# Six half-precision matmuls on a constant ahead of each group of neighbour sums

## The reference, cut to what matters

```python
for l in range(2):                       # relational network
    W = einsum('rb,bio->rio', coeff[l], basis[l])      # 8 matrices of 256x256
    msg = (h @ W)[etype, src] * norm                   # one row per edge
    h = segment_sum(msg, dst) + bias[l]                # relu after l == 0
x = layernorm(x + h)
h = x @ W_in + b_in
for l in range(3):                       # mean network
    h = relu(segment_mean(h[src], dst) @ W_agg[l] + h @ W_self[l] + b_hid[l])
out = layernorm(x + h @ W_out + b_out)
```

## Time and profile before

| what | value |
|---|---|
| median of 3 runs | 2405.6 us (2405.01 to 2408.9) |
| profiled execution, its own time | 2384.24 us |
| its span, first to last instruction | 2382.4 us |
| mean granted TensorE clock | 0.891 of full speed |
| busy: TensorE matmul, VectorE, GpSimd, ScalarE | 1794.9, 1202.8, 1254.7, 623.9 us |

### The profile page before, as it was taken

How to read it: one execution, slowest core, us unless ns; L and a number is a source line. 1 busy time by engine, 2 the same in 40 slices (tenths; PEclk the granted TensorE clock), 3 DMA queues, 4 the chain that set the end, 5 groups by cost and what they waited for, 6 DMA issues and landing times.

```text
span 2382.4 us, 29813 instructions
## 1 busy us (share of the span) xinstructions
PE 1794.9 (75%) x7693; PEld 1344.2 (56%) x7693; DVE 1202.8 (50%) x3964; ACT 623.9 (26%) x1520; POOL 1254.7 (53%) x1298
## 2 busy tenths in 40 slices
PE   3747777777677677757777777676676779999997
PEld 2435555555455455535555555455565567777776
DVE  4837745454455544335554555553368743232355
ACT  1112222222222222212322322322112124633332
POOL 5766666666666666366666666666666630000000
PEclk9978879989988898969798888988888889999999
DMA  6333333333333333233333333334533320000011
GB/s 199 87 91 98 101 98 98 100 101 98 102 97 99 101 98 99 65 95 100 104 103 101 103 103 100 104 102 121 171 105 100 95 59 11 1 1 1 1 35 44
DMA packets 118334, 208.03 MB, mean 87 GB/s; under 512 B 53668, under 2 KB 73908, under 8 KB 118168
## 3 DMA queue, kind: packets, MB, share of 16 engines
q0 software_dynamic: 62016, 169.04, 24.9%
q1 hardware_dynamic: 48848, 26.08, 3.8%
q10 hardware_dynamic: 7304, 10.96, 1.4%
HBM read 188.85 MB, written 17.13 MB: 86 GB/s over the span
## 4 chain that ended last, share of the span: by engine, by line
PE 49%; another core or an unknown queue 17%; DVE 14%; issue 13%; ACT 3%; DVEq 2%; POOL 1%; DMA 0%; ACTq 0%; SPq 0%; POOLq 0%
PE bank L657 15%; PE bank L823 11%; PE bank L610 9%; PE bank L645 4%; DVE RY L450 4%; DVE RY L441 3%; PE bank L588 2%; PE bank L840 2%; PE bank L768 2%; DVE RY L376 1%; DVE RY L375 1%; ACT RY L555 1%; ACT RY L489 1%; POOL RY L246 1%
## 5 line engine op out<-in xcount | busy, mean ns | idle before, releaser
L657 PE MATMUL bank<-RY 128*128 128x256 f32 x2580 | 870.6, 433 | 56.4 <-DVE RY L450 43.1
L246 POOL DMA_INDIRECT RY<-H,si x645 | 617.7, 958 | 354.1 <-issue 152.5
L246 POOL DMA_INDIRECT RY<-in_x,si x645 | 635.8, 986 | 313.9 <-issue 144.4
L441 DVE TENSOR_TENSOR RY<-RY,bank 128x256 f32 x430 | 180.9, 421 | 874.2 <-remote 629.5
L657 PEld LDWEIGHTS bank<-RY 128*128 128x128 f32 x2580 | 488.3, 220 | 164.1 <-DVE RY L450 54.2
L645 PE MATMUL bank<-idn,RY 128*128 128x128 f32 x860 | 194.8, 313 | 383.4 <-issue 206.9
L450 DVE TENSOR_SCALAR RY<-iot,c,wgt 128x128 f32<-128x128 f32 x1290 | 461.3, 369 | 1.3 <-issue 1.2
L555 ACT COPY RY<-bank 128x256 f32<-128x256 f32 x430 | 160.9, 374 | 984.1 <-PE bank L657 519.0
L645 PEld LDWEIGHTS bank<-idn,RY 128*128 128x128 f32 x860 | 119.8, 160 | 487.4 <-issue 414.6
L823 PE MATMUL bank<-Ar,hs 125*128 125x500 f32 x1200 | 305.8, 405 | 0.0
L823 PEld LDWEIGHTS bank<-Ar,hs 125*128 125x128 f32 x1200 | 225.7, 188 | 51.7 <-issue 9.2
(11 more groups left out here) (107 smaller groups left out, 1158.9 us busy)
## 6 DMA issues: line engine op xcount, KB each, us to landing
RY<-in_x,si POOLq DMA_INDIRECT x645
RY<-H,si POOLq DMA_INDIRECT x645
Ad<-RY SPq DMA_DIRECT2D x215, 40.0 KB
RX<-Ad ACTq DMA_DIRECT2D x20, 305.2 KB
RX<-in_basis ACTq DMA_DIRECT2D x2, 2048.0 KB, 30.0
H<-RY SPq DMA_DIRECT2D x22, 128.0 KB
RY<-in_x SPq DMA_DIRECT2D x22, 128.0 KB
X<-RY SPq DMA_DIRECT2D x22, 128.0 KB
```

What stands on the lines that cost most here:

```text
L246: e.indirect_dma_start(G[0:k, n % NG, :], None, table, bass.IndirectOffsetOnAxis(ap=si[0:k, t:t + 1], axis=0)).then_inc(s_land[n % NG], 16)
L441: e.tensor_tensor(o, o, bank[4 + wg % 2][:, 0:256].rearrange("p (q c) -> p q c", c=16), ALU.add).then_inc(s_za, 1)
L657: e.matmul(bank[2 + wg % 2][:, 0:256], S[0:k, n % NSL, :], G[0:k, n % NG, :], start=(i == 0), stop=(i == TA - 1)).then_inc(s_sum, 1)
```

## The change

Ahead of the first sum of each group, behind its three waits, stand six matmuls of the constant `iotN` (half precision, 0, 1, 2, ... in each row; written once at the start) with itself: 128x128 by 128x256, into the bank that the group's sums are about to fill. Each has `start=True`, and so has the first sum, which overwrites what they left. They signal nothing. The rest of the diff gives two waits of the general path semaphores of their own.

```diff
+FILL = 6
...
                     e.wait_ge(s_sel, n + 1)
                     e.wait_ge(s_land[n % NG], 16 * (n // NG + 1))
+                    if i == 0:
+                        for _ in range(FILL):
+                            e.matmul(bank[2 + wg % 2][:, 0:256], iotN[:, 0:128], iotN[:, 0:256], start=True, stop=True)
                     e.matmul(bank[2 + wg % 2][:, 0:256], S[0:k, n % NSL, :], G[0:k, n % NG, :], start=(i == 0),
                              stop=(i == TA - 1)).then_inc(s_sum, 1)
...
-        def pe_product(e, pairs, cols):
+        def pe_product(e, pairs, cols, done):
...
-            mm.then_inc(k_mm, 1)
+            mm.then_inc(done, 1)
...
-                take(e, k_x, 16)
+                take(e, k_xd, 16)
...
-                take(e, k_mm)
+                take(e, k_md)
```

More of the change, by code:

```diff
@@ L218, in program @@
         s_o, s_od = sem("s_o"), [sem(f"s_od{i}") for i in range(4)]
-        (k_start, k_own, k_ix, k_rows, k_prod, k_z, k_x, k_tr, k_ht, k_mm, k_cp, k_row, k_st, k_back, k_y, k_bn, k_sq, k_gather) = (
+        (k_start, k_own, k_ix, k_rows, k_prod, k_z, k_x, k_tr, k_ht, k_mm, k_cp, k_row, k_st, k_back, k_y, k_bn, k_sq, k_gather, k_xd, k_md) = (
             sem("k_" + n) for n in ("start", "own", "ix", "rows", "prod", "z", "x", "tr", "ht", "mm", "cp", "row", "st", "back",
-                                    "y", "bn", "sq", "gather"))
+                                    "y", "bn", "sq", "gather", "xd", "md"))
         def sp_setup(e):
@@ L1107, in pe_row @@
                 take(e, k_ht if c == 0 else k_cp)
-                pe_product(e, [(vh, W[:, :, c * 512:(c + 1) * 512])], 512)
+                pe_product(e, [(vh, W[:, :, c * 512:(c + 1) * 512])], 512, k_mm)
         def act_row(e):
@@ L1222, in pe_general @@
                 take(e, k_ht)
-                pe_product(e, [(vh, wts[:, 0, :, :])], 256)
+                pe_product(e, [(vh, wts[:, 0, :, :])], 256, k_md)
             for l in range(3):
@@ L1231, in pe_general @@
                     take(e, k_ht)
-                    pe_product(e, [(vh, wts[:, 1 + 2 * l, :, :]), (vh2, wts[:, 2 + 2 * l, :, :])], 256)
+                    pe_product(e, [(vh, wts[:, 1 + 2 * l, :, :]), (vh2, wts[:, 2 + 2 * l, :, :])], 256, k_md)
             with e.Fori(0, JB) as k:
@@ L1236, in pe_general @@
                 take(e, k_ht)
-                pe_product(e, [(vh, wts[:, 7, :, :])], 256)
+                pe_product(e, [(vh, wts[:, 7, :, :])], 256, k_md)
         def act_general(e):
@@ L1267, in sp_general @@
                 take(e, k_z)
-                e.dma_start(vz[0:PB, :], block(x, k)).then_inc(k_x, 16)
+                e.dma_start(vz[0:PB, :], block(x, k)).then_inc(k_xd, 16)
                 take(e, k_row)
@@ L1275, in sp_general @@
                     take(e, k_z)
-                    e.dma_start(vz[0:PB, :], block(H[l], k)).then_inc(k_x, 16)
+                    e.dma_start(vz[0:PB, :], block(H[l], k)).then_inc(k_xd, 16)
                     take(e, k_row)
@@ L1282, in sp_general @@
                 take(e, k_z)
-                e.dma_start(vz[0:PB, :], block(X1, k)).then_inc(k_x, 16)
+                e.dma_start(vz[0:PB, :], block(X1, k)).then_inc(k_xd, 16)
                 take(e, k_row)
```

## The result

The change made the kernel slower: 2429.93 us (2427.57 to 2431.66, 4 runs) against 2405.31 us (2404.51 to 2408.9, 4 runs), a ratio of 1.0096 with a 95% interval of 1.0084 to 1.0109. The prediction named 2388 us, faster; the time lies in its range, near the price of rival 1.

The account below looks back on a forecast made before the run. The prediction took late reports, which leave GpSimd without free slots, to bound the gather stage, not TensorE's throughput. Clock gain of -31 us and filler time of +14 us gave -17 us, from 2405.6 to 2388 us; range 2335 to 2445.

Parts of the forecast that it names:

- rival 1: Gather stage: fillers fall into prompt stretches and the clock does not recover; about +38 us, 2443 us, chance 0.32.
- What bounds the kernel: Gather stage: not TensorE's throughput; GpSimd runs out of its 16 slots because reports come late, then all go on together.
- Price of the fillers: TensorE, each group: 0.11 us a filler at full clock, 0.65 us for six, 280 us for 430 groups.
- cover: Gather stage: pauses of some 570 us take up the fillers' delay; only 5% of 280 us shows, +14 us.
- What they give back: Gather stage behind pauses: groups spared the half clock save 78 us of TensorE's time, counted as -31 us.
- half of the 80 escape: Of about 80 groups at 1.2 GHz half run at 2.4 GHz instead, 1.95 us less each, 78 us of TensorE's time.
- a weight of 0.4: Share of the 78 us saved right behind pauses that shows in the kernel's time; bounds 0 and 1.
- -31 + 14 = -17 us: Whole kernel: gain from the warmer clock plus what shows of the fillers' time, giving 2388 us.
- Rival 3: Gather stage: gathers and late reports alone set the pace, so nothing moves; 2406 us, give or take 4, chance 0.16.

Follow-up runs that it names:

- e17: Kernel before the change with 17 slots for gathered rows in place of 16: ratio 0.9994 on a chip with prompt reports.
- the first set: Runs on another chip, kernel before at 2384 us: three, six tiny and twelve fillers cost 0.51, 0.95 and 2.08%; six fillers moved ahead of the turn's waits, ratio 1.0135.
- e15: Kernel before, no fillers, twelve already fulfilled waits per group added to TensorE's stream: 2418.13 us against 2406.92, ratio 1.0039, late reports.
- e2: Changed kernel with its six fillers cut to 32 columns with 32 columns of weights: 2404.64 us, ratio 1.0095 to the kernel before.
- e1: Changed kernel with twelve fillers per group in place of six: 2433.03 us against 2384.03 for the kernel before, ratio 1.0208.
- e14: Changed kernel with six fillers of 512 columns in place of 256: 2438.51 us, ratio 1.0134 to the kernel before, late reports.
- e13: Changed kernel with twelve fillers in place of six, on a chip with late reports: 2461.8 us, ratio 1.0237 to the kernel before.
- e9: The change itself on a chip with prompt reports: 2116.42 us against 2116.39 for the kernel before, ratio 1.0001.
- e3: Changed kernel with its six fillers moved ahead of the waits of the turn: 2414.85 us, ratio 1.0135 to the kernel before.

## Why the prediction was wrong

**What bounds the kernel: right in half.** TensorE's throughput does not set the pace, and the late reports are real, since on chips without them the same kernel takes 2116 us. But the cycle was read wrongly. GpSimd running out of slots is an effect: with 18.3 us from a gather to its sum, TensorE's stream with its stops at the turn is what the stage waits for. This is read from traces; the run that would test it, e17, never met late reports. And not all engines resume together. TensorE went on because ScalarE had copied, and VectorE had resumed 2 us before both, in a row that the earlier trace rows leave out:

```profile
1733.22 0.42 DVE L441 TENSOR_TENSOR RY<-RY,bank 128x256 f32 x1 [5.39 <-remote]
```

The turn that it needed had ended at 1729.66, so its report was 3.6 us late, and the one for ScalarE 3.4 us: two reports late by about as much, one after the other.

**Price of the fillers: right.** 0.11 us each at full clock, measured so. Of their cover the runs show only the net with what the clock gives back.

**What they give back: wrong, and this is one of the two steps that failed.** The prediction said "I let half of the 80 escape" and "I give them a weight of 0.4". The first came about: the clock rose to 0.951, so the loss to half speed fell from 0.109 of the span to 0.049. The weight was far too high. Time and clock together were to give -31 + 14 = -17 us; the runs leave them between about 0 (the line of the first set) and +4 us (the split). The line of instructions, with e15 at 0.889, e2 at 0.917 and e1 at 0.980, needs no gain from the clock at all, though a small one that a like cost of time hides is not excluded. On a prompt chip the clock went up to 0.989 for nothing as well. The prediction had the row for it, 136 to 139 gathers in 200 us at clocks from 0.83 to 0.91, and set it aside as only a bound. 17 to 21 us of the error of 42 lie here.

**What an instruction costs: missing.** The sum had no term for the length of TensorE's stream. Shown: bare waits cost there, tiny fillers cost as much as full ones, and half the instructions at the same price in time cost 25 us less; 5160 instructions at 4.5 us per thousand are 23 us, the whole loss, and with the 17 to 21 us above they make up about the whole error. Not shown is the way. The fetches of TensorE's program rise with the loss, 71, 81, 91 and 111 blocks of 16 KB for before, e15, e14 and e13; 256 instructions at 4.6 ns are 1.2 us for each further block. That agrees with a fetch as the cause and as well with a cost in the handling of each instruction. The 55 gaps between fillers of e13 lie anywhere from 0.4 to 23 us after the start of the last fetch, all through the time between two; they are not tied to the moment of one. Waits in SyncE's stream on a chip with late reports would have told them apart, but were never run on one. The Trainium skill's page "Runtime: NRT & Kernel Launch", section "Instruction fetch mechanics", says that programs are fetched in blocks of 16 KB, 256 instructions, and that the cost of a block's boundary is mostly hidden. The block counts agree with the size; where reports are late, no run here shows the boundary hidden, and where they are prompt 20 more blocks cost nothing (e9).

**Rival 1** had the side, and nearly the time (2443 us) by luck: it laid the loss on TensorE's time and a clock that does not recover. **Rival 3** is what the prompt chips show, where the pace does come from the gathers alone.

**Open.** Why reports, and at times TensorE's instructions, are late on some chips; whether gathers, fetches or something outside the core hold them; why the fillers cost more ahead of the turn (e3). No version that still computes the right sums beat the kernel before on any chip.

## What to carry to other kernels

Before a fast clock is bought with extra work, find out whether the pace follows the clock at all: compare stretches of one trace at different clocks. If the pace is the same at 0.83 and 0.91, expect next to nothing from a warm array, even where the work that warms it is hidden. An engine that stops for a free slot is not yet the one that sets the pace: look how long its results lie unused. And work that is free in time is not free in instructions: try a tiny version of the same count and a wide version of half the count, which part the two with two runs.

## What the runs showed that I had not expected

The same kernel takes 2405 us beside the result, 2384 and 2407 us in the first and the fourth set, and 2115 to 2116 us on the three prompt chips (whether the 2405 and the 2407 are of one chip is not on record), and the change's effect goes with it: +0.96% on the first, none on one of the latter (interval -0.08 to +0.11%). The difference is in how soon TensorE's semaphore increments are seen, a median of 0.09 against 1.6 us after a sum, not in any engine's speed: a gather takes 0.95 us and a sum matmul 0.216 us between starts on both. An instruction more in TensorE's stream cost 4.5 to 4.8 ns where increments were late (3.6 ns for a bare wait), though the engine was idle for a quarter of the time. Twelve fillers without a wait between them came up to 2.0 us apart there. And in e2 matmuls of 32 columns by 32 started 0.25 us before the next sum for all six, less than 0.05 us each.
